# A graph layer on one core: the branch put behind the output products, degrees by products with ones, edge columns made later, third tile turned inside the fourth tile's sums

## The chip, the cores and the metric

The kernel runs on 1 core of one Trainium2 chip. The metric is the device time of one execution in microseconds (us). TensorE (PE) multiplies and transposes, VectorE (DVE) and ScalarE (ACT) work on vectors, GpSimd (POOL) does a little at the start, and SyncE (SP) starts the transfers. Each engine carries out its own instructions in the order of the program, and waits for others by semaphores.

## The reference, cut to what matters

A graph of 1250 nodes with 512 features and 20,000 edges sorted by target. One layer:

```
h    = relu(layernorm(x))
xn   = batchnorm(h)
agg  = segment_sum(xn[src], dst) / max(deg, 1)        # deg = edges that end at a node
conv = relu(agg @ W_conv + b_conv)
qf, kf = random features of the heads of h @ Wq, h @ Wk   (first 256 nodes; 8 heads)
attn = (qf (kf^T v)) / (qf . sum kf), then @ Wo
out  = x + batchnorm(conv + attn + h)
```

## The kernel before, in words

Nodes lie in 10 tiles of 128 rows, the last of 98. The features of the last phase lie turned: 4 tiles f of 128 features by 1250 nodes, and the nodes in three chunks c of 512, 512 and 226 (`CHUNKS`).

**Start.** x comes in and is normalized (`ln_stats`, `ln_scale` on VectorE, `ln_tile` on ScalarE). TensorE turns it tile by tile (`transpose_h`), and ScalarE copies the result out of the bank (`store_hT`). TensorE makes q and k (`qk`), features of them (`features`), and `project_consts` turns some vectors. `edge_values` on VectorE makes from gathered edge lists the two numbers of each edge; `columns` turns them on TensorE and waits for them (`g_ready`). `weight_sums` waits for `wabs_ready` (`weight_sizes` and `constants` on VectorE), and `bn_piece` takes the moments of hT.

**Middle.** For 25 groups of 10 windows of 5 target nodes, VectorE makes one-hot matrices (`one_hots`), TensorE multiplies them into counts of edges (`count`), and ScalarE stores these as A16 (`store`). In between TensorE projects the nodes by the scaled W_conv (`project`, bank G), which is split in a high and a low 16-bit part (`high_part` on ScalarE, `low_part` on VectorE), and does the attention: `attention(i)`, `attn_norm` on VectorE, `attn_T` on TensorE, `attn_copy` on ScalarE, and `heads_out`, the output products with Wo.

**The branch.** `uncovered_edges` loads a flag into a register of TensorE and jumps over a long body of products that runs only for edges that the windows don't cover. With this input the body is never run. VectorE has a branch of its own ahead of `last_phase`.

**Last phase.** `aggregate(f, c)` multiplies 20 times (10 source tiles, high and low part) into one bank. VectorE's `y(f, c)` scales by the inverse degrees `rdeg`, adds, and takes moments; `moments`, a square root on ScalarE and `scale` give the factors of tile f, ScalarE applies them (line 592), TensorE turns the tile (`transpose_z`, which waits for `z_act`), VectorE adds x (`finish`), and SyncE sends it out. The degrees come from `source_sum` on VectorE, which adds A16 over its 10 tiles into `asum`.

Eight banks take turns by the lists `order` and `order_end`: `pe_open` makes TensorE wait until the bank's last use was read.

Of the kernel before, what the change touches and what calls it, by code (L numbers as in the profile page):

```python
# [14 lines left out]
P = 128  # L15
# [5 lines left out]
FT = D // P  # L21
# [20 lines left out]
SLOW_LINKS = 8  # L42
EP, EJ = 125, E // 125
# [10 lines left out]
def gnn_kernel(nc, x, src, dst, g1, b1, g2, b2, w_conv, b_conv, w_q, w_k, w_v, w_o, proj, out):  # L54
    with ExitStack() as ctx:
# [3 lines left out]
        def sem(name):  # L59
# [96 lines left out]
        dcol = sb("dcol", [P, NT], F32)  # L156
# [28 lines left out]
        order = [("first",), ("hT", 0), ("hT", 1), ("q", 0), ("q", 1), ("hT", 2), ("hT", 3), ("hT", 4), ("hT", 5),  # L185
# [6 lines left out]
                 ("attn", 1), ("attnT", 0), ("attn", 3), ("attnT", 1), ("ha", 0), ("ha", 1)]  # L192
        order_end = [("agg", 0, 0), ("dcol",), ("agg", 0, 1), ("rdeg", 0), ("rdeg", 1), ("rdeg", 2), ("agg", 0, 2)]
        for f in range(1, FT - 1):
            order_end += [("agg", f, 0), ("agg", f, 1)] + [("zT", f - 1, j) for j in range(3)] + [("agg", f, 2)]
        order_end += [("agg", FT - 1, c) for c in range(3)] + [("zT", f, j) for f in (FT - 2, FT - 1) for j in range(3)]
        uses = {}
        nuse = [0] * 8
        for k, name in enumerate(order):
            b = 2 + k % 6  # L200
            if name == ("ha", 0):
                before_ha = list(nuse)
            nuse[b] += 1
            uses[name] = (b, nuse[b])
        for k, name in enumerate(order_end):
# [73 lines left out]
        dcol_ready = sem("dcol_ready")  # L279
# [23 lines left out]
        def _(sp):  # L303
# [25 lines left out]
            for f in range(FT):  # L329
                c = slice(f * P, (f + 1) * P)  # L330
                for j in range(2 if f < FT - 1 else 1):
                    stored(sp, "zT", f, j)
                    sp.dma_start(out[512 * j:512 * (j + 1), c].rearrange("(t p) n -> p t n", p=P),
                                 xs[:, 4 * j:4 * (j + 1), c]).then_inc(o_out, 16)
                stored(sp, "zT", f, 2)
                for i in range(8, NT if f < FT - 1 else 9):
                    sp.dma_start(out[i * P:i * P + rows_of(i), c], xs[0:rows_of(i), i, c]).then_inc(o_out, 16)
# [34 lines left out]
        def _(act):  # L372
# [57 lines left out]
            qk(0, 0)  # L430
            act.wait_ge(ln_ready, 3)
# [4 lines left out]
            store_hT(2)  # L436
            store_hT(3)
            qk(0, 1)
            store_hT(4)
            store_hT(5)  # L440
            edge_columns()
# [4 lines left out]
            store_hT(9)  # L446
            def store_v(t):
# [113 lines left out]
            store()  # L561
            attn_copy(0)
            store()
            high_part(9)
            while stores[0] < NGRP:
                store()
            attn_copy(1)
            ha_bias(0)
# [5 lines left out]
            for c, (c0, cn) in enumerate(CHUNKS):  # L574
                acc = landed(act, "rdeg", c)
                act.activation(rdeg[:, c0:c0 + cn], acc[:, 0:cn], ACT.Copy).then_inc(read("rdeg", c), 1)  # L576
            def copy_turned(f, j):
# [913 lines left out]
```

## Time and profile before

| | |
|---|---|
| median of 3 runs | 194.08 us (193.65 to 194.21) |
| the profiled execution | 194.64 us, span 192.2 us |
| TensorE busy | 171.7 us, 89% of the span |
| VectorE busy | 129.5 us, 67% |
| ScalarE busy | 90.0 us, 47% |
| mean granted TensorE clock | 0.968 of full speed |
| chain that ended last | TensorE 77%, issue 7%, VectorE 4%, transfers 4% |

### The profile page before, as it was taken

How to read it: one execution, taken by the hardware profiler on the slowest of the kernel's cores; microseconds unless marked ns; L12 is line 12 of the kernel's file. 1: busy time of each engine (PE TensorE's matmuls, PEld its weight loads, DVE VectorE, ACT ScalarE, POOL GpSimd, SP SyncE). 2: the span in 40 equal slices, each digit the busy share in tenths (PEclk: the TensorE clock that was granted, in tenths of full speed). 3: DMA queues.
4: the chain of work that ended last, by engine and by line, in shares of the span. 5: the costliest groups of instructions: out<-in, count | busy, mean ns of one | idle time of the engine just before them, and what ended most of it. 6: DMA issues, size and time to landing. Idle time of an engine off the chain costs nothing.

```text
span 192.2 us, 3020 instructions
## 1 busy us (share of the span) xinstructions
PE 171.7 (89%) x1131; PEld 117.3 (61%) x1132; DVE 129.5 (67%) x309; ACT 90.0 (47%) x162; POOL 7.5 (4%) x22
## 2 busy tenths in 40 slices
PE   0489879999999999999999999199999999999990
PEld 0468758765467465566767777078467474564870
DVE  3786495999583857899657663970306987596662
ACT  3257944447793649997505315202905122204050
POOL 5081000000000000000000000000000000000000
PEclk9999979999999999999999999669999999999997
DMA  5989900000070000000000000000086004031045
GB/s 182 387 256 310 354 22 0 0 0 3 2 235 0 0 3 0 0 5 0 0 3 0 0 3 0 3 3 0 0 285 251 0 0 133 3 100 35 0 122 146
DMA packets 11883, 13.69 MB, mean 71 GB/s; under 512 B 1458, under 2 KB 6748, under 8 KB 11868
## 3 DMA queue, kind: packets, MB, share of 16 engines
q1 hardware_dynamic: 10476, 12.13, 19.4%
q10 hardware_dynamic: 1072, 1.10, 1.7%
q0 software_dynamic: 320, 0.26, 0.6%
q8 instruction: 10, 0.16, 0.4%
q14 instruction: 5, 0.04, 0.1%
HBM read 10.92 MB, written 2.56 MB: 70 GB/s over the span
## 4 chain that ended last, share of the span: by engine, by line
PE 77%; issue 7%; DVE 4%; DMA 4%; ACT 3%; POOL 2%; POOLq 1%; DVEq 0%; ACTq 0%
PE bank L944 22%; PE bank L684 17%; PE bank L617 5%; PE bank L727 5%; PE bank L638 4%; DMA r<-in_dst,rows 4%; PE bank L708 4%; PE bank L698 4%; PE bank L661 3%; PE bank L629 3%; PE bank L672 2%; PE bank L652 2%; PE bank L975 2%; POOL r L365 1%; PE bank L992 1%
## 5 line engine op out<-in xcount | busy, mean ns | idle before, releaser
L684 PE MATMUL bank<-wc,xs 128*128 128x512 f32 (+1 forms) x80 | 38.6, 609 | 0.2 <-DVE gl L1212 0.2
L944 PE MATMUL bank<-r,gl 128*128 128x512 f16 (+1 forms) x120 | 38.2, 338 | 0.0
L944 PE MATMUL bank<-r,gh 128*128 128x512 f16 (+1 forms) x120 | 38.1, 339 | 0.0
L1075 DVE TENSOR_TENSOR ohb<-iota,bcol 128x1280 f16<-128x1280 f16 x25 | 20.4, 817 | 4.2 <-PE bank L629 4.1
L684 PEld LDWEIGHTS bank<-wc,xs 128*128 128x128 f32 (+1 forms) x80 | 13.6, 187 | 10.9 <-issue 10.9
L386 ACT ACTIVATE r<-bank 128x500 f16<-128x500 f32 x25 | 18.6, 770 | 3.0 <-PE bank L629 3.0
L617 PE MATMUL bank<-hT,r 128*128 128x256 f32 x64 | 18.0, 447 | 0.7 <-issue 0.7
L944 PEld LDWEIGHTS bank<-r,gl 128*128 128x128 f16 x120 | 11.7, 97 | 9.2
L944 PEld LDWEIGHTS bank<-r,gh 128*128 128x128 f16 x120 | 11.6, 97 | 9.1
L617 PEld LDWEIGHTS bank<-hT,r 128*128 128x128 f32 x64 | 14.3, 228 | 3.7 <-ACT hT L377 1.1
L1351 DVE SCALAR_TENSOR_TENSOR r<-bank,cinv,r 128x512 f32<-128x512 f32 (+1 forms) x12 | 7.7, 646 | 12.8 <-ACT r L576 6.8
L629 PEld LDWEIGHTS bank<-ohv,ohb 128*128 128x128 f16 x250 | 9.8, 97 | 7.5 <-issue 6.1
L1212 DVE SCALAR_TENSOR_TENSOR gl<-bank,gh 128x512 f16<-128x512 f32 (+1 forms) x10 | 6.9, 689 | 8.5 <-ACT gh L495 8.5
L727 PE MATMUL bank<-qe,wvo 128*128 128x256 f32 x32 | 8.7, 441 | 4.2 <-issue 4.2
L495 ACT ACTIVATE gh<-bank 128x512 f16<-128x512 f32 (+1 forms) x10 | 6.1, 608 | 13.3 <-PE bank L684 13.3
L727 PEld LDWEIGHTS bank<-qe,wvo 128*128 128x128 f32 x32 | 7.2, 227 | 5.6 <-issue 4.4
L629 PE MATMUL bank<-ohv,ohb 128*128 128x50 f16 x250 | 10.4, 184 | 0.0
L1075 DVE TENSOR_TENSOR ohv<-iota,vcol 128x500 f16<-128x500 f16 x25 | 10.3, 410 | 0.0
L587 ACT ACTIVATE bw<-mv,epst 128x1 f32<-128x1 f32 x4 | 1.2, 292 | 19.4 <-DVE mv L1362 19.4
L455 ACT ACTIVATE xs<-hT,t,s 128x384 f32<-128x384 f32 (+2 forms) x12 | 7.9, 753 | 2.6 <-DVE t L1149 2.6
L592 ACT ACTIVATE r<-r,t,s 128x512 f32<-128x512 f32 (+2 forms) x12 | 7.5, 689 | 3.0 <-DVE t L1376 3.0
L397 ACT ACTIVATE xs<-xs,lnw 128x512 f32<-128x512 f32 x10 | 7.4, 802 | 2.1 <-DVE lnw L1054 2.1
(175 smaller groups left out, 271.8 us busy)
## 6 DMA issues: line engine op xcount, KB each, us to landing
xs<-in_x SPq DMA_DIRECT2D x15, 256.0 KB, 4.9
out<-xs SPq DMA_DIRECT2D x7, 256.0 KB
r<-in_L_gnn_Wq SPq DMA_DIRECT2D x1, 1024.0 KB, 7.3
r<-in_L_gnn_Wk SPq DMA_DIRECT2D x1, 1024.0 KB, 5.9
wc<-in_L_gnn_W_conv SPq DMA_DIRECT2D x1, 1024.0 KB, 8.6
wvo<-in_L_gnn_Wv SPq DMA_DIRECT2D x1, 1024.0 KB, 10.7
wvo<-in_L_gnn_Wo SPq DMA_DIRECT2D x1, 1024.0 KB, 5.3
xs<-in_x ACTq DMA_DIRECT2D x3, 256.0 KB, 4.3
```

The lines of the kernel that those rows point to most:

```text
L386: act.activation(A16[:, :, p * GW * W:(p + 1) * GW * W].rearrange("p a (q d) -> p q a d", q=GW), bank[p % 2][:, 0:GW * NT * W].rearrange(" ...
L455: act.activation(xnT[:, f, a:b], hT[:, f, a:b], ACT.Identity, bias=t1[:, f:f + 1], scale=s1[:, f:f + 1]).then_inc(xn_ready, 1)
L617: last = nc.tensor.matmul(acc[:, t * NA:(t + 1) * NA], w[:, f, c:c + P], hT[:, f, 0:NA], start=(f == 0), stop=(f == FT - 1))
L629: last = nc.tensor.matmul(bank[p % 2][:, q * NT * W:(q + 1) * NT * W], ohb[:, s, :], ohv[:, s, :], start=True, stop=True)
L638: last = nc.tensor.matmul(acc[:, :], hT[:, f, t * P:(t + 1) * P], wvo[:, f, :], start=(f == 0), stop=(f == FT - 1))
L684: last = nc.tensor.matmul(acc[0:n, :], xnT[:, f, i * P:i * P + n], wc[:, f, :], start=(f == 0), stop=(f == FT - 1))
L698: last = nc.tensor.matmul(acc[:, j * (DH + 1):(j + 1) * (DH + 1)], kf[:, t, h, m * P:(m + 1) * P], v1[:, t, h, :], start=(t == 0), stop=(t ...
L708: last = nc.tensor.matmul(acc[:, j * (DH + 1):(j + 1) * (DH + 1)], qfT[:, m, h, t * P:(t + 1) * P], kv[:, m, h, :], start=(m == 0), stop=( ...
L727: last = nc.tensor.matmul(acc[:, t * NA:(t + 1) * NA], wvo[:, c, o:o + P], attnT[:, c, :], start=(c == 0), stop=(c == FT - 1))
L944: last = nc.tensor.matmul(acc[:, 0:cn], gg[0:n, s, f * P:(f + 1) * P], A16[0:n, s, c0:c0 + cn], start=(s == 0 and gg is gh), stop=(s == NT ...
L1075: last = V.tensor_tensor(oh[:, s0:s0 + n, :].rearrange("p s (m t) -> p s m t", t=2), iota16[:, 0:size].rearrange("p (m t) -> p m t", t=2). ...
L1351: V.scalar_tensor_tensor(out=yT[:, f, c0:c0 + cn], in0=sums, scalar=cinv[:, f:f + 1], in1=rdeg[:, c0:c0 + cn], op0=ALU.mult, op1=ALU.mult) ...
```

## The change

Five things move.

1. **Start, TensorE:** the second half of q goes behind the tiles 2 to 5 of h, and `columns` and `weight_sums` go behind the first key features. On ScalarE the copies of these tiles go ahead of `ln_tile(6)` to `(9)` and `edge_columns` behind the copy of tile 9; on VectorE `bn_piece(0)` and `constants` go ahead of `edge_values`.
2. **End of the middle:** `project(9, ..)` goes behind the counts, its second half behind `attn_T(1)`.
3. **The branch** goes behind `heads_out`.
4. **Degrees:** 10 products of one column, a copy to `dcol`, 10 products that spread it and three copies on ScalarE are replaced by three products of a matrix of ones with `asum` (all rows get the degree), three evictions on VectorE and one reciprocal of 128x1250, all ahead of the first sums.
5. **End:** the third tile was turned behind all sums, with x added by a product (`turn_with_residual`) and the copies on ScalarE and VectorE; now `transpose_z(2)` stands between the last two chunks of the fourth tile's sums, and VectorE's `finish` adds x. Ahead of the last turn stand 16 products (`LATE`) whose result is written over.

The core of the diff:

```
-        order_end += [("agg", FT - 1, c) for c in range(3)] + [("zT", f, j) for f in (FT - 2, FT - 1) for j in range(3)]
+        order_end += [("agg", FT - 1, 0), ("agg", FT - 1, 1)] + [("zT", FT - 2, j) for j in range(3)] + [("agg", FT - 1, 2)]
+        order_end += [("zT", FT - 1, j) for j in range(3)]
...
             attn_T(0)
-            count()
-            project(9, 1)
             attention(3)
             while counts[0] < NGRP:
                 count()
+            project(9, 0)
             attn_T(1)
-            uncovered_edges()
+            project(9, 1)
             pe.wait_ge(wo_in, 16)
             for i in range(2):
                 stored(pe, "attnT", i)
             heads_out(0)
             heads_out(1)
+            uncovered_edges()
...
+                    if (f, j) == (FT - 1, 0):
+                        for k in range(LATE):
+                            nc.tensor.matmul(acc[:, :], cone[:, :], A16[:, 0, 0:512], start=True, stop=True)
...
+            pe.wait_ge(asum_ready, 3)
+            for c, (c0, cn) in enumerate(CHUNKS):
+                acc = pe_open(pe, "deg", c)
+                nc.tensor.matmul(acc[:, 0:cn], cone[:, :], asum[:, c0:c0 + cn], start=True, stop=True).then_inc(full("deg", c), 1)
             for i in range(NT):
                 stored(pe, "G", i)
             aggregate(0, 0)
-            acc = pe_open(pe, "dcol")
-            pe.wait_ge(asum_ready, 3)
-            for t in range(NT):
-                last = nc.tensor.matmul(acc[:, t:t + 1], asum[:, t * P:(t + 1) * P], cone[:, 0:1], start=True, stop=True)
-            last.then_inc(full("dcol"), 1)
             aggregate(0, 1)
-            pe.wait_ge(dcol_ready, 1)
-            for c in range(3):
-                acc = pe_open(pe, "rdeg", c)
-                for t in range(4 * c, min(4 * c + 4, NT)):
-                    o = (t - 4 * c) * P
-                    last = nc.tensor.matmul(acc[:, o:o + P], dcol[:, t:t + 1].to_broadcast([P, P]), ident[:, :],
-                                            start=True, stop=True)
-                last.then_inc(full("rdeg", c), 1)
             aggregate(0, 2)
-            for f in range(1, FT - 1):
+            for f in range(1, FT):
                 aggregate(f, 0)
                 aggregate(f, 1)
                 transpose_z(f - 1)
                 aggregate(f, 2)
-            for c in range(3):
-                aggregate(FT - 1, c)
-            turn_with_residual(FT - 2)
             transpose_z(FT - 1)
...
             def last_phase(slow):
+                for c, (c0, cn) in enumerate(CHUNKS):
+                    acc = landed(dve, "deg", c)
+                    V.tensor_scalar(rdeg[:, c0:c0 + cn], acc[:, 0:cn], 1.0, None, ALU.max).then_inc(read("deg", c), 1)
+                for c in range(3):
+                    stored(dve, "deg", c)
+                link(V.reciprocal(rdeg[:, :], rdeg[:, :]))
                 stored(dve, "ha", 0)
                 stored(dve, "ha", 1)
                 V.tensor_tensor(hT[:, :, 0:NA], hT[:, :, 0:NA], haT[:, :, :], ALU.add).then_inc(r_head, 1)
...
                 y(f, 0)
                 y(f, 1)
+                finish(f - 1, 0)
                 link(y(f, 2))
                 moments(f)
+                finish(f - 1, 2)
                 scale(f)
...
-                acc = landed(dve, "zT", f - 1, 2)
-                V.tensor_copy(xs[:, 8:NT, (f - 1) * P:f * P], acc[:, 0:(NT - 8) * P].rearrange("p (t n) -> p t n", t=NT - 8)
-                              ).then_inc(read("zT", f - 1, 2), 1)
+                finish(f - 1, 1)
                 for j in range(3):
                     finish(f, j)
```

How the instructions stand on TensorE at the start, before (L609 turns h, L617 is `qk`, L785 and L787 are `columns`, L795 is `weight_sums`, L661 the features):

```order
L609 MATMUL bank<-ident,xs 128x128 x8
L617 MATMUL bank<-hT,r 128x256 x16
L609 MATMUL bank<-ident,xs 128x128 x16
L776 MATMUL bank<-ident,pj 128x128 x2
L777 MATMUL bank<-ident,vrow 128x20
L785 MATMUL bank<-ident,r 128x125 x4
L787 MATMUL bank<-ones,nout 1x1 x2
L617 MATMUL bank<-hT,r 128x256 x8
L609 MATMUL bank<-ident,xs 128x128 x16
L795 MATMUL bank<-gh 128x512 x4
L661 MATMUL bank<-pT,r 128x256 x4
L652 MATMUL bank<-half,r 128x2 x4
```

and after the change, where the same lines are L597, L605, L773, L775, L783 and L649:

```order
L597 MATMUL bank<-ident,xs 128x128 x8
L605 MATMUL bank<-hT,r 128x256 x8
L597 MATMUL bank<-ident,xs 128x128 x16
L764 MATMUL bank<-ident,pj 128x128 x2
L765 MATMUL bank<-ident,vrow 128x20
L605 MATMUL bank<-hT,r 128x256 x16
L597 MATMUL bank<-ident,xs 128x128 x16
L649 MATMUL bank<-pT,r 128x256 x4
L773 MATMUL bank<-ident,r 128x125 x4
L775 MATMUL bank<-ones,nout 1x1 x2
L783 MATMUL bank<-gh 128x512 x4
L640 MATMUL bank<-half,r 128x2 x4
```

The columns stood ahead of k; now they stand behind k, four turns and the first features, and the second half of q has taken the place behind the turns.

On TensorE around the branch, before (L708 is `attention`, L629 `count`, L719 `attn_T`, L684 `project`; L733 and L734 are the flag and the jump, over a body of 190 products to the 16 of L727, `heads_out`):

```order
L708 MATMUL bank<-kv,r 128x65 x8
L719 MATMUL bank<-ident,qe 128x128 x4
L629 MATMUL bank<-ohv,ohb 128x50 x10
L684 MATMUL bank<-wc,xs 98x512 x2
L708 MATMUL bank<-kv,r 128x65 x8
L629 MATMUL bank<-ohv,ohb 128x50 x10
L719 MATMUL bank<-ident,qe 128x128 x4
L733 TENSOR_LOAD flag
L733 ISA x2
L734 COMPARE_AND_BRANCH
```

and after the change (L696, L617, L707, L672; L715 is `heads_out`, L721 and L722 the flag and the jump, and what it jumps to are the products for the degrees, L958):

```order
L617 MATMUL bank<-ohv,ohb 128x50 x10
L707 MATMUL bank<-ident,qe 128x128 x4
L696 MATMUL bank<-kv,r 128x65 x8
L617 MATMUL bank<-ohv,ohb 128x50 x10
L672 MATMUL bank<-wc,xs 98x512 x2
L707 MATMUL bank<-ident,qe 128x128 x4
L672 MATMUL bank<-wc,xs 98x512 x2
L715 MATMUL bank<-qe,wvo 128x256 x16
L721 TENSOR_LOAD flag
L721 ISA x2
L722 COMPARE_AND_BRANCH
```

The last projection now fills the places ahead of and behind the last attention turn, and the output products stand ahead of the jump.

On VectorE behind its branch, after the change (L1298 evicts the degrees, L1301 inverts them, L1304 adds the attention to h, L1315 is the first instruction of `y`):

```order
L1298 TENSOR_SCALAR r<-bank 128x512 x2
L1298 TENSOR_SCALAR r<-bank 128x226
L1301 RECIPROCAL r<-r 128x1250
L1304 TENSOR_TENSOR hT<-hT,haT 128x4x256
L1315 SCALAR_TENSOR_TENSOR r<-bank,cinv,r 128x512
```

Before, the last phase began with the addition to h, and only 128x10 values were inverted here.

## Rows read from the trace of the kernel before

**Rows 1.** Chain that ended last, early: start us, length us, what.

```profile
26.17 5.34 PE bank L617 x16
...
36.17 3.56 PE bank L617 x16
```

**Rows 2.** Timeline, TensorE, early: start, length, line, op, tiles, count, [idle before].

```profile
25.36 0.65 PE L785 MATMUL bank<-ident,r 125*128 125x125 f32 x4 [1.93 <-DVE r L1102]
```

**Rows 3.** Timeline, VectorE, early.

```profile
21.46 0.29 DVE L1089 TENSOR_SCALAR r<-r 125x256 int32<-125x256 int32 x1 [3.51 <-DMA r<-in_dst,rows]
...
25.49 2.47 DVE L1061 BATCH_NORM_STATS2 st<-hT 128x6 f32<-128x512 f32 x4 [0.19 <-issue]
...
33.91 3.65 DVE L1061 BATCH_NORM_STATS2 st<-hT 128x6 f32<-128x512 f32 x8 [2.13 <-ACT hT L377]
...
40.97 0.80 DVE L1075 TENSOR_TENSOR ohb<-iota,bcol 128x1280 f16<-128x1280 f16 x1
```

**Rows 4.** Timeline, ScalarE, early.

```profile
17.88 0.60 ACT L403 ACTIVATE qT<-bank 128x512 f32<-128x512 f32 x1 [0.93 <-PE bank L617]
...
23.97 1.07 ACT L377 ACTIVATE hT<-bank 128x512 f32<-128x512 f32 x2
```

**Rows 5.** Windows A:B: length, busy us of five engines, PEclk, DMA share, GB/s.

```profile
26.00:28.00 2.00, 2.00 (x10) 1.60 (x10) 2.00 (x5) 1.09 (x3) 0.00 (x0) 0.55 0.05 12
126.00:128.00 2.00, 2.00 (x6) 1.63 (x5) 1.79 (x5) 0.00 (x0) 0.00 (x0) 0.50 0.00 0
128.00:130.00 2.00, 2.00 (x9) 1.68 (x8) 0.64 (x2) 0.00 (x0) 0.00 (x0) 0.85 0.00 0
```

**Rows 6.** Chain that ended last, from attention(3) to the end of the sums.

```profile
119.87 0.72 issue
...
134.12 4.32 PE bank L944 x20
138.44 0.23 PE bank L984 x10
...
143.01 2.23 PE bank L992 x20
...
155.82 1.09 PE bank L975 x10
...
168.59 12.52 PE bank L944 x80
```

**Rows 7.** Timeline, TensorE, at the branch.

```profile
125.38 8.74 PE L727 MATMUL bank<-qe,wvo 128*128 128x256 f32 x32 [4.17 <-issue]
```

**Rows 8.** DMA queues, window 122.0:122.5: packets, MB, share of 16 engines.

```profile
q8 instruction: 1, 0.02, 15.7%
```

**Rows 9.** Lines by form, VectorE reciprocals: shape, count, busy us, mean ns.

```profile
L1370 DVE RECIPROCAL bw<-bw 128x1 f32<-128x1 f32 x4 | 0.7, 164 | 0.8 <-ACT bw L587 0.5
L1230 DVE RECIPROCAL zr<-zz 128x4 f32<-128x4 f32 x4 | 0.7, 178 | 0.1
L1338 DVE RECIPROCAL dcol<-dcol 128x10 f32<-128x10 f32 x1 | 0.2, 217 | 0.0
```

**Rows 10.** Timeline, VectorE, last phase.

```profile
128.40 0.28 DVE L1193 TENSOR_TENSOR asum<-r 128x226 f16<-128x226 f16 x1
135.09 1.23 DVE L1334 TENSOR_TENSOR hT<-hT,haT 128x1024 f32<-128x1024 f32 x1 [6.42 <-ACT haT L471]
...
145.89 0.75 DVE L1351 SCALAR_TENSOR_TENSOR r<-bank,cinv,r 128x512 f32<-128x512 f32 x1 [6.77 <-ACT r L576]
...
183.75 0.16 DVE L1370 RECIPROCAL bw<-bw 128x1 f32<-128x1 f32 x1 [0.49 <-ACT bw L587]
...
186.83 1.62 DVE L1386 TENSOR_TENSOR xs<-bank,xs 128x512 f32<-128x512 f32 x3 [0.79 <-PE bank L975]
```

**Rows 11.** Timeline, ScalarE, last phase.

```profile
153.21 1.99 ACT L592 ACTIVATE r<-r,t,s 128x512 f32<-128x512 f32 x3 [1.00 <-DVE t L1376]
...
184.73 0.60 ACT L580 ACTIVATE xs<-bank 128x512 f32<-128x512 f32 x1 [1.01 <-PE bank L958]
```

More of the change, by code:

```diff
@@ L42 @@
 SLOW_LINKS = 8
+LATE = 16
 EP, EJ = 125, E // 125
@@ L330, in _ @@
                 c = slice(f * P, (f + 1) * P)
-                for j in range(2 if f < FT - 1 else 1):
+                for j in {FT - 2: (0, 2, 1), FT - 1: (0, 2)}.get(f, (0, 1, 2)):
                     stored(sp, "zT", f, j)
[L333 to L337, printed above, removed]
+                    if j < 2:
+                        sp.dma_start(out[512 * j:512 * (j + 1), c].rearrange("(t p) n -> p t n", p=P),
+                                     xs[:, 4 * j:4 * (j + 1), c]).then_inc(o_out, 16)
+                    else:
+                        for i in range(8, NT if f < FT - 1 else 9):
+                            sp.dma_start(out[i * P:i * P + rows_of(i), c], xs[0:rows_of(i), i, c]).then_inc(o_out, 16)
             sp.wait_ge(src_in, 16)
@@ L561, in _ @@
             store()
+            store()
             attn_copy(0)
-            store()
-            high_part(9)
             while stores[0] < NGRP:
@@ L567, in _ @@
             attn_copy(1)
+            high_part(9)
             ha_bias(0)
@@ L826, in _ @@
             project_consts()
-            columns()
+            qk("q", wq, 1)
             pe.wait_ge(wk_in, 16)
@@ L837, in _ @@
             features("uk", kT, 0)
+            columns()
+            weight_sums()
             diagonal(0, 0)
@@ L918, in _ @@
             attention(2)
-            project(9, 0)
             count()
             attention(1)
+            count()
             attn_T(0)
-            count()
-            project(9, 1)
             attention(3)
@@ L946, in aggregate @@
                 last.then_inc(full("agg", f, c), 1)
-            def turn_with_residual(f):
-                for j in range(3):
-                    acc = pe_open(pe, "zT", f, j)
-                    pe.wait_ge(z_act, 3 * f + j + 1)
-                    tiles = range(4 * j, min(4 * j + 4, NT))
-                    for i in tiles:
-                        pe.wait_ge(x_in[i], 32)
-                    for i in tiles:
-                        n, o = rows_of(i), (i - 4 * j) * P
-                        nc.tensor.matmul(acc[:, o:o + P], yT[:, f, i * P:(i + 1) * P], ident[:, :], start=True, stop=False)
-                        last = nc.tensor.matmul(acc[0:n, o:o + P], ident[0:n, 0:n], xs[0:n, i, f * P:(f + 1) * P],
-                                                start=False, stop=True)
-                    last.then_inc(full("zT", f, j), 1)
             def transpose_z(f):
@@ L1240, in _ @@
             ln_scale(2)
+            bn_piece(0)
+            constants()
             edge_values()
-            bn_piece(0)
             weight_sizes()
-            constants()
             bn_piece(1)
@@ L1334, in last_phase @@
                 V.tensor_tensor(hT[:, :, 0:NA], hT[:, :, 0:NA], haT[:, :, :], ALU.add).then_inc(r_head, 1)
-                acc = landed(dve, "dcol")
-                V.tensor_scalar(dcol[:, :], acc[:, 0:NT], 1.0, None, ALU.max).then_inc(read("dcol"), 1)
-                stored(dve, "dcol")
-                V.reciprocal(dcol[:, :], dcol[:, :]).then_inc(dcol_ready, 1)
-                for c in range(3):
-                    stored(dve, "rdeg", c)
                 if slow:
```

49 lines of the change are left out of this document (15 added, 34 removed), and 13 rows, old and new, of the table order.

## The prediction, made before the changed kernel was run

> **What bounds the kernel now.** I read the page first (TensorE busy for 89% of the span, the other engines for two thirds or less), then the chain that ended last, which lies on TensorE for 77%, and then what TensorE was idle or slow for. Four places stand out, and the change touches each. At the start TensorE waits 1.93 us ahead of the columns for VectorE's edge values [rows 2]. After this wait the granted clock is near its lower level, 0.55 in 26 to 28 us [rows 5], and the first half of k takes 5.34 us where the second half, the same work, takes 3.56 [rows 1]. Behind the last count it waits 0.72 us for the last attention norm [rows 6]. Between the last attention turn and the output products it is idle for 4.17 us at "issue" [rows 7]: that is the jump over the unused body, and in this gap a 16 KB packet of instructions arrives [rows 8]. The gap too is followed by the lower clock: 0.50 until 128 us and 0.85 in the next 2 us [rows 5], so it rose at about 128.6 us, 3.2 us after work began again; half of 3.2 is 1.6, and the output products (twice the work of a half of k) take 8.74 us against 2 x 3.56 = 7.12 [rows 7, 1], also 1.62.
>
> **Start.** The instructions of TensorE up to the second half of k are the same as before, in another order. If no wait is left, the wait and the slow clock go: 1.93 + 1.78 = 3.7 us, and the second half of k begins at 36.17 - 3.7 = 32.5. What could be late is VectorE. The first half of q is there at 17.88 [rows 4]; the turns of tiles 2 and 3 end about 1 us later, ScalarE is busy with q until 19.1 and copies a tile in 0.53 (1.07 for two) [rows 4], so tile 3 is copied at 20.2. Then VectorE takes the moments, 2.47 [rows 3], the constants (estimate 1.6), and the edge values, which took from 21.46 to 25.4 [rows 3]: done at about 28.2. TensorE comes to the columns about 2.6 us (columns, weight sums, diagonal) ahead of 32.5, at 29.9: 1.7 us to spare. The weight sizes end about 30.7, where TensorE wants them at 30.7: a wait of 0 to 0.4. On VectorE the gaps of 3.51, 0.19 and 2.13 us [rows 3] shrink to one of some 2.4 behind the layer norm, so the first one-hot matrices, at 40.97 now, begin at 40.97 - 3.3 = 37.7 and are there a microsecond ahead of the first count. Both engines come forward by 3.2 to 3.7. **Term: -3.5** (from -3.7 down to -1.9, if the clock sinks at some other short wait).
>
> **End of the middle.** Up to the output products the set of instructions is again the same. The last projection is cut so that its halves lie behind the last count (cover for the last norm) and behind the last turn (1.8 us of cover for ScalarE's copy of 0.6). The wait of 0.72 goes. The output products follow without a gap, at the full clock; they end at 134.12 - 0.72 - 4.17 - 1.62 = 127.6 on the old scale.
>
> **The branch** costs what it cost, only later: a gap of 4.17 us and then 1.6 us lost to the low clock, now on the degrees and the first sums. In it lies nothing that has to be waited for otherwise (VectorE's source sums ended at 128.7 [rows 10], and come some 2.5 us earlier because the norms do). So moving it gains nothing by itself: the gap's old cover, the copy of 0.6 us, was inside it. The gap could be shorter: ahead of the jump stood a turn that had just waited, now stand 32 records of dense work, and the sequencer may come to the flag before they end. From -1.5 for that to +0.5; I take 0, since no row shows how far it runs ahead.
>
> A rule on this: the Trainium skill, page "Runtime: NRT & Kernel Launch", section "Instruction fetch mechanics", says that a taken branch to a target outside the two fetched blocks of 256 instructions stalls for a fetch. By that rule, the trace agrees: the gap holds such a packet. The same section gives TensorE a store of 2048 instructions; by that figure neither kernel would stall here, and the trace shows 4.17 us.
>
> **Degrees.** Removed from TensorE: 0.23 and 2.23 us [rows 6]. Added: 1250 columns of 16-bit products; a sum of 20 x 512 columns takes 4.32 [rows 6], so 0.53. **Term: -0.72 - 2.46 + 0.53 = -2.65**, with the norm's wait. What is new lies on VectorE, ahead of everything in the last phase: three evictions and a reciprocal of 1250 elements a row. The nearest rows: 178 ns for 4 elements, 217 for 10 [rows 9], 6.5 ns an element, so 8.3 us; a plain instruction with 1024 elements takes 1.23 [rows 10], so 1.5 us is the lower end. I take 8.3, because its own rows grow. Let B be the first product behind the branch. VectorE has the degrees evicted at about B + 2.3, inverted at B + 10.6, and has added the attention (1.23) at B + 11.8, the start of y(0, 0). From there to the first applied chunk of tile 0 it takes 153.21 + 0.66 - 145.89 = 8.0 us [rows 10, 11]: B + 19.8. TensorE wants it behind sum (1, 1), at B + 0.53 + 1.6 + 10.58 + 8.64 = B + 21.35 (two sums of 4.32 and one of 1.94 a tile). That leaves 1.5 us: the reciprocal is hidden up to 9.8 us, and from there costs one for one. VectorE was late in the same way before (y(0, 0) began at 145.89, after a wait of 6.77 [rows 10]) and caught up.
>
> **End.** Let T be the end of sum (3, 1), 179.17 now (181.11 less 1.94 [rows 6]); the last VectorE instruction ends at 188.45 = T + 9.28 [rows 10]. Added in this path: the turn of the third tile, 1.09 [rows 6], now stands ahead of the last sum, which ends at T + 3.03, and VectorE, free at T + 2.2 before, starts y(3, 2) 0.85 later; its gap takes the first of the third tile's additions (0.65 of the 1.62 for three [rows 10]). A short addition (0.35) stands ahead of the factors. Removed: the root's 0.49 [rows 10], late because ScalarE was copying the third tile, and some 0.5 of ScalarE's second copy at 184.73 [rows 11], which held the application of the factors. Sum +0.2. The 16 late products take 16 x 0.216 = 3.5, to T + 6.5; the first applied piece comes at T + 6.9, so they cost nothing, and keep TensorE busy. The 3.4 us of turning with x are off the path: ScalarE's copies waited for them, but the factors came at nearly the same time. Output transfers start in another order; the last ones are the same. **Term: +0.2** (-0.5 to +1).
>
> **Sum.** -3.5 - 2.65 + 0.2 = -5.95. The profiled execution took 194.64, so 188.7; it lies 0.56 above the median of 194.08. Forecast 188.1.
>
> **Rivals.**
> - *Part of the start is given back.* VectorE is dense from 38 us on, and the edge columns, now copied ahead of the key features on ScalarE, could hold the one-hot matrices. It would give back 1.5 to 3.5 us: 189.6 to 191.6. Against it: both engines come forward by nearly the same. Chance 0.15.
> - *The gap shrinks or goes.* If the sequencer runs ahead, 186 to 187. If the jump lands in a block that is there already, as the skill's page on the runtime would have it for a near target, the gap and its low clock go too: 188.1 - 5.8 = 182.3. Worked out from the code the jump is as long as before (a body of 190 products, more than a block, each with its weight load), so a fetch is likelier. Chances 0.12 and 0.04.
> - *The reciprocal decides: slower.* On VectorE ahead of y(0, 0), price one for one above 9.8 us. It eats the gain of 5.95 at 15.8 us, 12.6 ns an element, twice what the rows say; at 20 us the kernel would take 198. For it: one reciprocal row has at most 10 elements. Chance 0.04.
> - *No change*: half of the start given back, and a reciprocal of some 13.5 us; 188.1 + 2.0 + 3.7 = 193.8. Chance 0.02.
>
> The forecast itself, 187.0 to 189.6, has 0.63. A measurement of this kernel can tell about 0.3% from no change. Faster 0.94, same 0.02, slower 0.04. The range of 186.0 to 191.0 leaves out the short jump, most of a slow reciprocal, and the worst of the first rival.
>
> **What would show it.** In the changed profile: no wait of TensorE ahead of the columns and a granted clock of 1.00 at 26 to 30 us; the second half of k at 32.5; output products of 7.1 us, then a gap of about 4.2 us with a packet of instructions, and 0.50 behind it; a reciprocal of 8 us and no wait of TensorE ahead of the first `transpose_z`; the last sum's end at 179.17 - 6.15 + 3.03 = 176.05. Wrong it would be made by a wait of TensorE between 38 and 110 us, a reciprocal over 10 us, or a gap of another length.

## The result: 183.12 us, faster than the range allowed

| | before | after |
|---|---|---|
| median | 194.11 us (193.65 to 194.21) | 183.12 us (182.90 to 183.39, 4 runs) |
| the profiled execution | 194.64 us, span 192.2 us | 183.13 us, span 181.3 us |
| mean granted TensorE clock | 0.968 | 0.991 |

After over before is 0.9439, with a 95% interval of 0.942 to 0.9459. The prediction said 188.1, with a range of 186.0 to 191.0: the sign was right, and the size too small by 5 us.

The page of the changed kernel: parts 1 and 2, with the span in 40 slices.

```profile
span 181.3 us, 2928 instructions
PE 167.1 (92%) x1090; PEld 111.3 (61%) x1091; DVE 139.1 (77%) x313; ACT 87.6 (48%) x157; POOL 7.6 (4%) x22
PE   0469999999999999999999999999999999999980
...
PEclk9999999999999999999999999999999999999996
```

TensorE is now without a hole from the fourth slice on, and its granted clock stays at the upper level until its last products. VectorE has 10 us more work than before (139.1 for 129.5), and yet behind the start TensorE waits for it only once, for 0.2 us in the middle.

The timeline of TensorE at the start, as in [rows 2]; L773 turns the columns, L783 is `weight_sums`.

```profile
12.44 6.24 PE L605 MATMUL bank<-hT,r 128*128 128x256 f32 x16 [0.74 <-issue]
20.75 7.17 PE L605 MATMUL bank<-hT,r 128*128 128x256 f32 x32
30.66 0.65 PE L773 MATMUL bank<-ident,r 125*128 125x125 f32 x4
31.64 0.81 PE L783 MATMUL bank<-gh 128*128 128x512 bf16 x3 [0.16 <-issue]
```

The wait for the columns (1.93 before) is gone, and the second half of q with the first half of k takes 7.17 us at a granted clock of 1.00. The second half of k begins at 33.24 in the chain of waits, against 36.17 [rows 1].

The chain that ended last, from the last attention turn (L707) over the last half projection (L672), the output products (L715) and the degrees (L958) to the sums (L932) and turns (L952).

```profile
115.33 0.44 PE bank L707 x4
115.77 1.72 PE bank L672 x4
117.48 6.91 PE bank L715 x32
124.39 0.37 issue
124.76 0.69 PE bank L958 x3
...
125.49 19.38 PE bank L932 x100
144.87 1.09 PE bank L952 x10
...
169.31 1.95 PE bank L932 x20
```

What to see: "issue" at the jump is 0.37 us. In [rows 7] it was 4.17, and in the forecast it was still to be 4.17. The output products take 6.91 instead of 8.74.

Windows of the changed kernel around the jump, as in [rows 5]: length, busy us of PE, PEld, DVE, ACT and POOL, PEclk, DMA share, GB/s.

```profile
122.00:124.00 2.00, 2.00 (x11) 1.75 (x10) 0.69 (x3) 0.00 (x0) 0.00 (x0) 1.00 0.03 8
124.00:126.00 2.00, 1.59 (x8) 0.53 (x7) 0.83 (x2) 1.54 (x3) 0.00 (x0) 1.00 0.03 8
126.00:128.00 2.00, 2.00 (x11) 0.89 (x10) 1.87 (x3) 2.00 (x3) 0.00 (x0) 1.00 0.00 0
```

The granted clock is 1.00 on both sides of the jump. A packet of instructions still comes. This is the DMA part of the window 122.0:122.5.

```profile
q8 instruction: 1, 0.02, 11.5%
```

It now comes while TensorE is still at the output products, 2.1 us ahead of their end at 124.39. Before, a packet came in the same window [rows 8], but TensorE was already idle and stayed so until 125.38. The last thing ahead of the jump that TensorE's sequencer has to wait for is ScalarE's copy of the last attention turn:

```profile
115.80 0.60 ACT L466 ACTIVATE qe<-bank 128x512 f32<-128x512 f32 x1 [1.45 <-PE bank L707]
```

It ends at 116.4, 5.8 us ahead of the packet.

The timeline of VectorE in the last phase: evictions, reciprocal, the addition of the attention, and the first `y`.

```profile
125.17 1.59 DVE L1298 TENSOR_SCALAR r<-bank 128x512 f32<-128x512 f32 x3 [2.41 <-PE bank L958]
126.89 7.97 DVE L1301 RECIPROCAL r<-r 128x1250 f32<-128x1250 f32 x1
134.89 1.23 DVE L1304 TENSOR_TENSOR hT<-hT,haT 128x1024 f32<-128x1024 f32 x1
136.03 0.74 DVE L1315 SCALAR_TENSOR_TENSOR r<-bank,cinv,r 128x512 f32<-128x512 f32 x1
```

And that of ScalarE, where tile 0 is applied:

```profile
143.33 1.99 ACT L580 ACTIVATE r<-r,t,s 128x512 f32<-128x512 f32 x3 [1.00 <-DVE t L1340]
```

The reciprocal took 7.97 us (forecast 8.3). The first of three applied chunks of tile 0 is there at about 144.0, and TensorE comes to its turn at 144.87: some 0.9 us to spare, and no wait.

**Where the time came from**, by the two traces:

| place | before | after | gain |
|---|---|---|---|
| second half of k begins | 36.17 | 33.24 | 2.93 |
| wait for the last attention norm | 0.72 | none | 0.72 |
| gap at the jump | 4.17 | 0.37 | 3.80 |
| output products | 8.74 | 6.91 | 1.83 |
| degrees on TensorE | 0.23 + 2.23 | 0.69 | 1.77 |
| end, from sum (3, 1) to the last VectorE instruction | 9.28 | 9.41 | -0.13 |

The sum is 10.92, and the spans differ by 10.9. The forecast had 0 for the third and fourth line together, which are 5.63.

### The profile page after: what moved, and what is told of

The parts are those of the page before. It is cut to its first block, busy times and chain, and to the rows that moved or that the text cites. A ratio compares the mean times of both kernels' runs of the same rounds, so it can differ in the third digit from the quotient of the medians.

```text
span 181.3 us, 2928 instructions
## 1 busy us (share of the span) xinstructions
PE 167.1 (92%) x1090; PEld 111.3 (61%) x1091; DVE 139.1 (77%) x313; ACT 87.6 (48%) x157; POOL 7.6 (4%) x22
## 3 DMA queue, kind: packets, MB, share of 16 engines
HBM read 10.92 MB, written 2.56 MB: 74 GB/s over the span
## 4 chain that ended last, share of the span: by engine, by line
PE 85%; DVE 6%; ACT 3%; DMA 2%; issue 2%; DVEq 0%; ACTq 0%
PE bank L932 23%; PE bank L672 18%; PE bank L605 9%; PE bank L626 4%; PE bank L696 4%; PE bank L686 4%; PE bank L715 4%; PE bank L649 4%; PE bank L617 3%; PE bank L597 3%; PE bank L660 2%; PE bank L952 2%; DMA edst<-in_dst 2%; PE bank L640 2%; DVE xs L1350 1%
## 5 line engine op out<-in xcount | busy, mean ns | idle before, releaser
L672 PE MATMUL bank<-wc,xs 128*128 128x512 f32 (+1 forms) x80 | 38.6, 608 | 0.1
L932 PE MATMUL bank<-r,gl 128*128 128x512 f16 (+1 forms) x120 | 38.2, 338 | 0.0
L932 PE MATMUL bank<-r,gh 128*128 128x512 f16 (+1 forms) x120 | 38.1, 339 | 0.0
L672 PEld LDWEIGHTS bank<-wc,xs 128*128 128x128 f32 (+1 forms) x80 | 13.6, 187 | 10.8 <-issue 10.8
L605 PE MATMUL bank<-hT,r 128*128 128x256 f32 x64 | 17.1, 430 | 0.7 <-issue 0.7
L932 PEld LDWEIGHTS bank<-r,gh 128*128 128x128 f16 x120 | 11.6, 97 | 9.6 <-issue 0.4
L932 PEld LDWEIGHTS bank<-r,gl 128*128 128x128 f16 x120 | 11.7, 97 | 9.2
L605 PEld LDWEIGHTS bank<-hT,r 128*128 128x128 f32 x64 | 13.7, 218 | 3.4 <-issue 1.1
L617 PEld LDWEIGHTS bank<-ohv,ohb 128*128 128x128 f16 x250 | 9.8, 98 | 6.9 <-issue 5.5
L1315 DVE SCALAR_TENSOR_TENSOR r<-bank,cinv,r 128x512 f32<-128x512 f32 (+1 forms) x12 | 7.7, 644 | 5.3 <-PE bank L932 5.3
L617 PE MATMUL bank<-ohv,ohb 128*128 128x50 f16 x250 | 10.4, 184 | 0.0
L1026 DVE BATCH_NORM_STATS2 st<-hT 128x6 f32<-128x512 f32 (+1 forms) x12 | 6.1, 580 | 3.0 <-ACT hT L377 3.0
L686 PEld LDWEIGHTS bank<-v,r 128*128 128x128 f32 x64 | 7.6, 192 | 1.0 <-issue 1.0
```

What stands on the lines that cost most here:

```text
L605: last = nc.tensor.matmul(acc[:, t * NA:(t + 1) * NA], w[:, f, c:c + P], hT[:, f, 0:NA], start=(f == 0), stop=(f == FT - 1))
L617: last = nc.tensor.matmul(bank[p % 2][:, q * NT * W:(q + 1) * NT * W], ohb[:, s, :], ohv[:, s, :], start=True, stop=True)
L672: last = nc.tensor.matmul(acc[0:n, :], xnT[:, f, i * P:i * P + n], wc[:, f, :], start=(f == 0), stop=(f == FT - 1))
L686: last = nc.tensor.matmul(acc[:, j * (DH + 1):(j + 1) * (DH + 1)], kf[:, t, h, m * P:(m + 1) * P], v1[:, t, h, :], start=(t == 0), stop=(t ...
L932: last = nc.tensor.matmul(acc[:, 0:cn], gg[0:n, s, f * P:(f + 1) * P], A16[0:n, s, c0:c0 + cn], start=(s == 0 and gg is gh), stop=(s == NT ...
L1315: V.scalar_tensor_tensor(out=yT[:, f, c0:c0 + cn], in0=sums, scalar=cinv[:, f:f + 1], in1=rdeg[:, c0:c0 + cn], op0=ALU.mult, op1=ALU.mult) ...
```

## The experiments

Theory A was formed from these rows: TensorE's sequencer runs ahead of the products. It reads the flag and asks for the code behind the jump as soon as it has come past its last real wait. So the stall, the idle time at the jump, is hidden by whatever dense work stands between this wait and the jump. ("Sequencer" is the part of the engine that reads its instructions and does the waits and jumps.) The main rivals: a jump costs the same wherever it stands (the forecast); and the place of jump and target in the code decides, since a target whose code has been fetched already needs no fetch. In the expectations A is the theory of running ahead, and the other letters are rivals of it. Each group ran on one chip beside the kernel before, whose medians there were 194.0 to 194.6 us; ratios are to it. The changed kernel itself ran only with the result and, as e12, beside e9, e10 and e11, so in the other groups differences from its 183.12 us are between chips, and some tenths of a us in them mean nothing. No kernel here leaves out anything of the reference; the added products are written over.

### The branch alone, and the branch put back

**e1_branch_only** is the kernel before with only the call moved:

```
             attn_T(1)
-            uncovered_edges()
...
             heads_out(0)
             heads_out(1)
+            uncovered_edges()
```

> The kernel before with the branch alone put behind the output products; nothing else moves. Theory A, the sequencer runs ahead of the products and reaches the jump while they still run: the gap falls from 4.17 us to about 0.4 us, now behind the output products, the granted clock stays at 1.00 (1.6 us), and the copy of the last attention turn, 0.65 us, comes out from under the gap: 194.1 - 3.8 - 1.6 + 0.65 = 189.3 us. Theory B, the jump costs 4.2 us wherever it stands (the forecast's): 194.1 + 0.65 = 194.7 us.

Measured: 190.44 us (188.82 to 192.34), ratio 0.9802 (0.9666 to 0.9939), so faster by 0.6 to 3.3%. The timeline of its TensorE at the two places (L726 output products, L943 the first sum):

```profile
122.61 7.14 PE L726 MATMUL bank<-qe,wvo 128*128 128x256 f32 x32 [0.89 <-ACT qe L464]
130.66 0.38 PE L943 MATMUL bank<-r,gh 128*128 128x512 f16 x1 [0.90 <-ACT haT L470]
```

Moving one call by itself is worth some 3.6 us by the medians. The traces are sharper: from the last attention turn to the first sum TensorE takes 9.57 us (121.09 to 130.66), where it took 13.37 (120.58 to 133.95), 3.8 less. What remains are two waits for copies of ScalarE of 0.9 us each; the first had been inside the gap before. The forecast's rule (theory B, 194.7 us) is wrong.

**e2_branch_back** is the changed kernel with the call ahead of the output products again, but still behind the last half projection:

```
             project(9, 1)
+            uncovered_edges()
             pe.wait_ge(wo_in, 16)
...
             heads_out(1)
-            uncovered_edges()
```

> The changed kernel with the branch alone put back ahead of the output products, behind the second half of the last projection. Theory A: what counts is how much work is queued on TensorE behind the last wait that really stopped the sequencer. There is no such wait for some 4 us ahead of the jump now, so the gap stays small, 0.3 to 1 us, and the time is 183 to 184 us. Theory C, only the dense output products hide the jump: gap about 4.2 us and the lower clock behind it, 183.1 + 3.8 + 1.6 = 188.5 us. Theory D, the place of the jump in its block of instructions decides: the place is again that of before, 188.5 us as well.

Measured: 183.82 us (183.54 to 184.44), ratio 0.9508 (0.9418 to 0.9598). Its timeline:

```profile
114.86 0.60 PE L708 MATMUL bank<-ident,qe 128*128 128x128 f32 x4
115.30 1.88 PE L673 MATMUL bank<-wc,xs 128*98 128x512 f32 x4
118.93 7.14 PE L716 MATMUL bank<-qe,wvo 128*128 128x256 f32 x32 [1.75 <-issue]
```

The jump now has 2.3 us of work between the last wait (for the norm, ahead of the turn L708) and itself, and the gap is 1.75, with the products behind it at full speed. The packet came at 115.95, while L673 was at work. So most of the gain does not need the branch behind the output products: with the half projection in front of it the gap is already less than half of the 4.17, and behind what is left of it the clock did not fall in this trace.

### A wait put back ahead of the jump

**e3_wait_ha0** and **e4_wait_ha1** add to the changed kernel a wait for ScalarE's copy of the first or of the second output bank, right ahead of the jump. The values are there in any case, and only the sequencer is held.

```
             heads_out(1)
+            stored(pe, "ha", 0)        # e4: "ha", 1
             uncovered_edges()
```

> The changed kernel with one wait ahead of the flag: TensorE's sequencer waits until ScalarE has read the first half of the output products (about 2.5 us ahead of the second half's end). Theory A: the sequencer comes to the jump some 1.3 us later than now, the instruction packet comes at about 123.5 instead of 122.2, and the gap grows from 0.37 to about 1.7 us: 184.4 us. Theory D (place in the block): the same as the changed kernel, 183.1 us, since one wait moves the place by one instruction at most.

> The changed kernel with a wait ahead of the flag for ScalarE's reading of all output products, about 0.9 us behind their end. Theory A: nothing runs ahead, so the gap is 0.9 plus some 4.2 us, about 5 us, and the lower clock behind it costs 1.6 us more: 183.1 + 4.7 + 1.6 = 189.4 us. Theory D: only the wait's own 0.9 us: 183.7 us.

Measured: e3 184.08 us (four of six between 183.65 and 184.12, two at 186.4 and 186.6), ratio 0.9516 (0.9431 to 0.9601); e4 189.59 us (188.12 to 189.81), ratio 0.9797 (0.9708 to 0.9886). The timeline of e3, whose profiled execution is of the 186 kind, and windows of it:

```profile
126.64 0.69 PE L959 MATMUL bank<-asum,cone 128*128 128x512 f16 x3 [1.88 <-issue]
...
126.00:128.00 2.00, 1.32 (x6) 0.49 (x7) 0.94 (x2) 2.00 (x3) 0.00 (x0) 0.91 0.03 8
128.00:130.00 2.00, 2.00 (x6) 0.73 (x5) 1.87 (x3) 1.98 (x3) 0.00 (x0) 0.50 0.00 0
```

The chain of e4:

```profile
116.27 6.92 PE bank L715 x32
...
123.22 0.85 ACT haT L472 x2
124.06 4.45 issue
128.51 1.20 PE bank L959 x3
```

One wait that is met anyway costs 6.5 us by the medians (5.0 between the two profiled executions, of which this one had a first half of q 1.0 us shorter). It releases the sequencer at 124.06; the packet comes at 125.9, and the first product behind the jump starts at 128.51. Then the clock is at 0.51 in 128 to 130 us, and three degree products take 1.20 instead of 0.69. This is the stall of [rows 7] again, at the new place. In e3 the sequencer is released when the first bank's copies are done, at about 122.2 and so some 2.6 us ahead of the end of the output products, and the gap is 1.88. After it the clock fell in the execution that was profiled. The two groups of times suggest that it does so in some executions only: the mean granted clock was 0.984 and 0.983 in the two long ones and 0.994 to 0.996 in the others. Theory D as it is stated, 183.1 us for e3 and 183.7 for e4, is ruled out by e4.

Where a real wait stands shortly ahead of the jump (before, e2, e3, e4), the packet comes 1.9 to 2.1 us behind its release. In these kernels and in the changed one the first product behind the jump comes 2.5 to 3.0 us behind the packet. So theory A needs one correction. In the changed kernel the packet comes 5.8 us behind the last wait, and not 1.9: the sequencer did not get to the flag as soon as it was free. The packet is 2.1 to 2.2 us ahead of the end of the output products in the changed kernel and e1 alike, and also in e5, e6, e7, e8 and e12 below, with 7 us of products without a wait ahead of the jump in each. If it left the flag 1.9 us earlier here too (an estimate from the other traces), the sequencer was some 4.0 us ahead of the products in all seven. The stall from the flag to the first product, 1.9 + 2.5, is a little longer than that, and the rest is the gap of 0.37.

### The other parts, each put back

**e5_start_back** puts back the order of the start on the three engines, with the banks in their old turns (`columns()` and `weight_sums()` ahead of the key features, and so on).

> The changed kernel with the start alone as it was before (second half of q, columns, weight sums, copies, moments and constants in the old order). The comparison of the two traces puts 2.93 us on the start (second half of k at 33.24 instead of 36.17 us): 183.1 + 2.9 = 186.0 us. The forecast's size for it is 3.5 us: 186.6 us. Rival, the middle absorbs the start, since VectorE is dense there: 183.1 to 184 us.

Measured: 184.62 us (184.52 to 185.22), ratio 0.9524 (0.9457 to 0.9591). The start is worth 1.5 us here, half of the 2.93; in the timeline the second half of k begins at 34.69, where the changed kernel's timeline has 33.10, 1.59 later. The wait for the columns was only 1.07 us in this kernel's trace, and the clock didn't fall behind it: the first half of k took 3.72. **e10_start_only** gives the new start to the kernel before, and nothing else.

> The kernel before with the new start alone. The old start lost 1.93 us in the wait for the columns and 1.78 us in the low clock behind it. Putting the old start into the changed kernel cost only 1.5 us: there the wait was 1.07 us and the clock did not fall. Theory: the loss by the clock comes only in executions in which it falls in that wait, so the start alone is worth between 1.5 and 3.5 us: 190.6 to 192.6 us. Rival, the start is worth its full 3.5 us whenever nothing else is changed: 190.6 us or less.

Measured: 191.29 us (190.71 to 192.39), against 193.99 (190.85 to 195.82 in seven executions) for the kernel before: 2.7 us, and the two overlap, so this figure is a rough one. In the timeline the second half of k begins at 32.54, where the kernel before has 36.03: 3.49 us in the traces, close to the forecast's 3.5. So the start's worth depends on what the old start loses. By the traces that is 3.49 us where the wait was 1.93 and the clock fell behind it, and 1.59 where the wait was 1.07 and the clock stayed.

**e6_degrees_back** has the old degrees: one-column products, spread through `dcol`.

> The changed kernel with the degrees as before: 10 products of one column, the copy to dcol, 10 spreading products and three copies on ScalarE, and no long reciprocal. TensorE gets 0.23 + 2.23 us back and loses 0.69 us: 183.1 + 1.8 = 184.9 us. Rival, the long reciprocal on VectorE costs something now, so taking it away gives some of that back: 184 us or less.

Measured: 185.78 us (185.09 to 186.14 in three; a fourth execution took 444.71 and is left out), ratio 0.9567 (0.9469 to 0.9664): 2.7 us dearer than the whole change, where the two traces have 1.77. The rival, that the long reciprocal costs something, is ruled out. The rest shows at the first sum in its timeline:

```profile
125.52 0.38 PE L937 MATMUL bank<-r,gh 128*128 128x512 f16 x1 [1.13 <-ACT haT L474]
```

Without the degrees in between, the first sum stands directly behind the jump and waits for a bank that ScalarE is still emptying: 1.13 instead of 0.37. The three new products also cover this copy.

**e7_end_back** has the old end, with the third tile turned behind all sums. **e8_no_late** has `LATE = 0`.

> The changed kernel with the third tile turned behind all sums, x added to it by products and ScalarE's and VectorE's copies, as before, and without the 16 late products. From the end of the fourth tile's second sum to VectorE's last instruction the two traces have 9.28 us (before) and 9.41 us (changed): 183.1 - 0.1 = 183.0 us, no difference that can be measured. Rival, the end was worth 0.5 us or more and something else in the last phase lost as much: 183.6 us or more.

> The changed kernel without the 16 late products, so that TensorE idles some 4 us ahead of the last turn. If the clock falls in this gap as it did in the gap of the branch before, the turns run at half speed: the first four, on the path, take 0.4 us more, and the last ones are hidden: 183.5 us. Rival, the clock or the turns' speed does not matter: 183.1 us.

Measured: e7 182.73 us (181.89 to 183.37), ratio 0.9413 (0.9335 to 0.9491); e8 183.52 us (182.52 to 184.05), ratio 0.9445 (0.9365 to 0.9524). Both intervals take in the changed kernel's 0.9439: no difference that these times can tell. The forecast's +0.2 for the end fits, and so does 0. For the late products the traces say more. The last turn, in the changed kernel and in e8:

```profile
175.04 1.58 PE L952 MATMUL bank<-ident,r 128*128 128x128 f32 x10 [0.34 <-ACT r L580]
...
175.46 2.37 PE L952 MATMUL bank<-ident,r 128*128 128x128 f32 x10 [3.88 <-ACT r L580]
```

In e8 TensorE idles for 3.88 us, the granted clock is 0.50 in 176 to 178 us, and VectorE ends 6.9 us behind the last sum instead of 6.4. So the 16 products buy some 0.5 us, which is what the expectation had. The old end doesn't need them, because its turns with x keep TensorE at work and the clock at 1.00.

### Warm products, and the place in the code

In every trace so far the first half of q, ahead of which TensorE had hardly worked, takes 5.2 to 6.6 us, where 3.56 is the time of such a half later. **e9_warm** adds 56 products of ones with ones around the first turns, into a bank that is written over later:

```
+            warm(36)      # ones x ones, 128x128, ahead of the first turns
...
+            warm(14)      # and warm(6) further on, between turns and q
```

> The changed kernel with 56 extra products of 128x128 ones on TensorE in its idle times at the start (36 ahead of the first product, 14 ahead of the first turns, 6 ahead of q), results unused. Theory: the first half of q takes 5.3 to 6.6 us in the traces so far, where the same work takes 3.56 later, because the clock is still low; kept busy from the start, TensorE does it in 3.6 us, and the whole program comes forward by 2 to 2.7 us: 183.1 - 2.4 = 180.7 us. Rival, ScalarE and VectorE set the pace behind q, or the extra products delay the first turns: 182.5 us or more.

> The changed kernel once more, on the same chip as the three beside it, to compare them with and to see how its start varies: 183.1 us by every theory; the first half of q between 5.2 and 6.7 us.

> The kernel with the old end (the third tile turned behind all sums, no late products), which was within its noise of the changed kernel, and with the same 56 extra products at the start. If the old end is as good as the new one and the extra products are worth 2.4 us: 180.6 us, the same as the changed kernel with the extra products alone. If the old end is better by the 0.4 us between the medians: 180.2 us.

Measured, on one chip: e9 181.03 us (180.73 to 181.34); e12, the changed kernel once more, 182.62 (182.55 to 182.88); e11, the warm products with the old end, 181.51 (181.05 to 182.08). Timeline of e9:

```profile
12.16 4.26 PE L605 MATMUL bank<-hT,r 128*128 128x256 f32 x16
...
115.66 7.07 PE L715 MATMUL bank<-qe,wvo 128*128 128x256 f32 x32
122.56 0.69 PE L965 MATMUL bank<-asum,cone 128*128 128x512 f16 x3
```

This is the fastest version, 1.6 us ahead of the change. The first half of q takes 4.26 (5.40 in e12), which was meant. The gap at the jump is now nought (0.70 in e12), which was not: I had not thought of the jump at all. The packets came at 115.9, 120.7 and 124.9, so the jump was no longer followed by one that TensorE waited for. (e11 and e13, with the same products, have a first half of q of 5.10 and 4.98 us, so 4.26 is the best case.) The 56 products shift all that stands behind them in the code. Is it this place, or only the running ahead? **e13_warm_wait_ha1** is e9 with the wait of e4 in front of the jump, so that nothing can run ahead. **e14_before_warm** gives the 56 products to the kernel before.

```
             heads_out(1)
+            stored(pe, "ha", 1)        # e13, beside the warm products
             uncovered_edges()
```

> The kernel with the wait ahead of the flag for ScalarE's reading of all output products, in which nothing runs ahead of the jump (gap 5.34 us), now with the 56 extra products at the start, which are 112 instructions more ahead of the jump. If the jump's target then lies in a block that was fetched already, no packet is waited for: the gap is the wait of 0.9 us and what the flag and the jump take by themselves, some 2 us (in the runs before, the packet came 1.9 us behind the last wait), about 2.8 us in all, and the time about 184 us. If the place does not matter, the gap is again 5.3 us and the time 189.6 - 1.6 = 188 us.

> The kernel before with the 56 extra products at the start and nothing else. By the clock alone they are worth up to 1.6 us, less if the clock falls in the wait for the columns as before: 192.4 to 194 us, with the gap of 4.17 us at the jump as it was. If the place of the jump matters, it lies early in a block now and its target in the next one, fetched already: the gap falls to some 1.5 to 2 us and the time to 188.5 to 190.5 us.

Measured: e13 184.07 us (183.59 to 185.42), ratio 0.9472 (0.9418 to 0.9526). Its chain, to be laid beside that of e4:

```profile
116.23 6.92 PE bank L715 x32
...
124.02 1.52 issue
```

and the window behind the gap:

```profile
126.00:128.00 2.00, 1.98 (x11) 0.83 (x10) 1.87 (x4) 2.00 (x3) 0.00 (x0) 1.00 0.03 8
```

The same wait, met at nearly the same time (124.02 and 124.06), is followed by 1.52 us instead of 4.45. The next packet comes at 126.1, when TensorE is at work again since 125.54. So reading the flag and jumping takes 1.5 us, and the fetch the other 2.9; with the 56 products ahead the target is there already. The packets of the steady stream fit this: the last one ahead of the wait's release came at 116.3 in e13 and at 107.7 in e4, so that one block more had been fetched. By the Trainium skill, page "Runtime: NRT & Kernel Launch", section "Instruction fetch mechanics", a taken branch whose target is not in the current window of two blocks forces a fetch; the two traces agree, with 1.52 and 4.45 us for the two places.

e14 came out at 194.69 us (190.74 to 195.86 in ten executions), ratio 0.9967 (0.9751 to 1.0182): the time expected if the place matters was missed, and a small difference would not be seen. The kernel before spread from 191.1 to 197.4 on that chip. The timeline of its profiled execution, at 195.47 one of the longer ones:

```profile
26.19 1.09 PE L791 MATMUL bank<-ident,r 125*128 125x125 f32 x4 [3.33 <-DVE r L1109]
...
126.83 7.53 PE L727 MATMUL bank<-qe,wvo 128*128 128x256 f32 x25 [3.92 <-issue]
```

Two things show. The gap at the jump is 3.92, with a packet at 124.1: here the same shift does not bring the target into the fetched code. That excludes that the warm products by themselves take the stall away. The expectation had placed the jump early in a block, and that was wrong: the last packet ahead of it came at 107.5, 14.8 us before the turn's wait ends. This fits blocks too, but the borders of the blocks were not worked out, so that it is argued and not shown where a jump comes free. And what q gains (8.15 us for 32 records) goes into a longer wait for the columns, 3.33 instead of 1.93, because in the old order VectorE's edge values set that moment.

## Why the prediction was wrong

**The step that failed** is "The branch costs what it cost, only later: a gap of 4.17 us and then 1.6 us lost". It went in as 0, with a lower bound of -1.5, and came out at -5.63 (3.80 of the gap, 1.83 of the clock). The doubt was written down, "the sequencer may come to the flag before they end", with 186 to 187 as its price, and got 0.12. Two things were wrong in it. The choice of 0: e1 (one call moved, 3.6 us gained) and e4 (one wait added, the stall back at 4.45 us) show that the running ahead happens every time and decides the gap. And the bound: it counted a shorter gap, but kept the low clock behind it. A gap of 0.37 leaves the clock at 1.00, so the 1.83 go with it. Had I worked from what stood in front of the jump, the rows would have given more: [rows 6] have a wait of 0.72 at the turn right ahead of the old jump, so the sequencer had been held there and could not be ahead.

**The rival "the gap goes", 182.3**, came within 0.8 us of the result, but by luck: its reason was a target fetched already, and in the changed kernel the packet is fetched, and hidden. That reason is real too, as e13 shows; there it took 56 products more ahead of the jump.

**Start**, -3.5: it was -2.93. The mechanism was right (no wait, full clock at 26 to 28 us, VectorE in time), the size off by 0.6. The first half of q took 6.24 in this execution, where before it was 5.36 (8.92 for both halves, less the 3.56 that such a half takes later); this part varies from 5.2 to 6.6 between the traces, and no term of the forecast had it. In e10's trace, with 5.62 there, the new start gives 3.49. By the medians, undoing it costs 1.5 (e5) and adding it gives some 2.7 (e10).

**Degrees and the norm's wait**, -2.65: -2.49. The wait of 0.72 went as said; the three products took 0.69 for the forecast 0.53. **The reciprocal** was 7.97 for the forecast 8.3, 6.4 ns an element, hidden with 0.9 us to spare, and 1.5 forecast. The estimate of some 10 us from the Trainium skill's page "VectorE: DVE Perf Modes", section "First, the fixed hardware budget", was too high by 2. **End**, +0.2: +0.13, and e7 can't tell it from nothing. The late products were forecast to cost nothing and keep TensorE busy, and they did.

The misses add up: 5.63 more than forecast at the jump, 0.57 less at the start, 0.16 less at the degrees, 0.07 better at the end: 4.97. The measured median is 4.98 below 188.1.

**What stays open.** The lead of some 4.0 us is an estimate: the packet's 2.1 us ahead of the end of the output products and the 1.9 us that it comes behind a release elsewhere. It is the same in seven traces with more than that ahead of the jump, so it looks like a bound; what sets it, and whether it goes by time or by the number of instructions, was not tried. Whether a gap of 1.8 to 1.9 us brings the clock down is not settled: it did in [rows 5] behind 1.93 us and in e3's trace, did not in e2's behind 1.75, and not in e13's behind 2.41. Where the border lies among the 56 products, and which offsets of the jump are free, was not tried.

## What to carry to other kernels

Cost a jump by what stands between it and the last wait that its engine really has to sit out, and not by the gap that it shows where it is now. Here the flag was read some 4 us ahead of the end of the output products, which leaves 0.4 us of it, and one wait of a microsecond set directly ahead of it costs 6.5. Dense work beyond those 4 us hid no more: the changed kernel had 7 us of it. When a gap on TensorE can close, count the low clock behind it into the bound as well. And of two versions whose code differs in length ahead of a jump, one may be free of the fetch and the other not; compare with the wait in place before a reason is given.

## What the runs showed of the hardware that was not expected

- Counted from the end of the wait ahead of it, a jump of TensorE costs 4.45 us where its target must be fetched and 1.52 where it is there (e4 and e13), and nought where products without a wait stand ahead of it and the target is there too (e9).
- With products free of waits ahead of the jump, the packet comes 2.1 to 2.2 us ahead of their end in seven traces, however long ago the last wait was (5.8 us in the changed kernel).
- The granted clock reads 1.00 in the first slices of the changed kernel, while the first half of q takes 6.24 us where 3.70 is the later time; its longest records take 0.76 us, twice the later 0.38. With 56 small products ahead it took 4.26 (e9), 4.98 (e13) and 5.10 (e11), and in the last two the column does read 0.50 at 10 to 14 us. The column alone would have hidden this in the changed kernel.
- A long reciprocal on VectorE costs 6.4 ns an element, 7.97 us for 1250.
